# A four-layer conditional network on one core: rotated expert order, spills by block, spread routing

## The reference

```
x += MoE(x):   shared MLP 256->1024->256, gelu(gate)*up, plus the 2 of 8 experts that top-2 of softmax(cond) picks
x += x @ (sum_e cond[b,e] * W1[e] * mask).T + b1        one mixed 256x256 matrix per batch
x += x @ W_base.T + b_base + 2 * sum_e cond[b,e] * (x @ A[e].T) @ B[e].T        LoRA of rank 16
x += down[e](silu(up[e](x)+b) * (gate[e](x)+b)) + b,   e = argmax(cond[b]), hidden 512, 1 of 8 experts
```

## Time and profile before

| what | value |
| --- | --- |
| median of 3 runs | 1271.83 us (1269.04 to 1275.28) |
| the profiled execution's own time | 1274.07 us |
| its span | 1272.4 us |
| granted PE clock, mean | 0.987 of full speed |
| PE / PEld busy | 1224.9 / 1096.2 us |
| DVE / ACT / POOL busy | 643.9 / 476.4 / 476.5 us |
| chain that ended last | PE 84%, POOL 4%, SPq 4%, DVE 3%, issue 3%, DMA 2% |

### The profile page before, as it was taken

One profiled execution on the slowest core, in us unless ns is written; L12 is line 12 of the kernel. 1 busy time (PEld: TensorE's weight loads), 2 busy tenths in 40 slices (PEclk: granted clock), 3 DMA queues, 4 the chain that ended last, 5 costly groups with the idle time before them and its releaser, 6 DMA issues.

```text
span 1272.4 us, 29091 instructions
## 1 busy us (share of the span) xinstructions
PE 1224.9 (96%) x8000; PEld 1096.2 (86%) x8001; DVE 643.9 (51%) x1126; ACT 476.4 (37%) x889; POOL 476.5 (37%) x313
## 2 busy tenths in 40 slices
PE   7987999999999999999999999999999995999998
PEld 6987998888888888888888888999999984887787
DVE  6777575445445455454545454465555542433333
ACT  4354532232322223222322223343344332655554
POOL 2265589307144053260808260010000007888200
PEclk9998999999999999999999999999999997999999
DMA  7258993202112022130313120032233246444211
GB/s 216 61 171 246 278 266 92 67 12 81 47 46 82 14 64 62 33 95 16 95 33 95 44 68 15 19 146 92 99 105 118 85 146 209 148 131 142 64 49 41
DMA packets 130996, 123.82 MB, mean 97 GB/s; under 512 B 64512, under 2 KB 114944, under 8 KB 128896
## 3 DMA queue, kind: packets, MB, share of 16 engines
q1 hardware_dynamic: 114960, 56.56, 16.5%
q0 software_dynamic: 15984, 66.59, 16.1%
HBM read 97.42 MB, written 25.69 MB: 97 GB/s over the span
## 4 chain that ended last, share of the span: by engine, by line
PE 84%; POOL 4%; SPq 4%; DVE 3%; issue 3%; DMA 2%; ACT 1%; POOLq 0%; ACTq 0%; DVEq 0%
PE bank L572 14%; PE bank L573 14%; PE bank L574 14%; PE bank L925 6%; PE bank L624 5%; PE bank L626 5%; PE bank L625 5%; PE bank L609 5%; PE bank L946 3%; PE bank L789 2%; PE bank L668 2%; PE bank L670 1%; PE bank L669 1%; SPq L350 1%; POOL Wl L406 1%
## 5 line engine op out<-in xcount | busy, mean ns | idle before, releaser
L1443 DVE TENSOR_TENSOR FS<-bank,FS 128x512 f32<-128x512 f32 x200 | 138.1, 690 | 273.8 <-PE bank L574 237.5
L404 POOL TENSOR_TENSOR Wh<-raw,one 128x1024 fp32r<-128x1024 f32 x79 | 150.3, 1902 | 316.6 <-PE bank L626 283.4
L1002 ACT ACTIVATE FS<-bank 128x512 f32<-128x512 f32 x200 | 119.5, 597 | 328.7 <-PE bank L574 328.4
L572 PE MATMUL bank<-Wh,RS 128*128 (+1 forms) x576 | 227.0, 394 | 4.7 <-DVE Wl L1533 2.6
L573 PE MATMUL bank<-Wl,RS 128*128 (+1 forms) x576 | 226.5, 393 | 0.0
L574 PE MATMUL bank<-Wh,RS 128*128 (+1 forms) x576 | 225.0, 391 | 0.0
L406 POOL TENSOR_TENSOR Wl<-raw,Wh 128x1024 fp32r<-128x1024 f32 x79 | 191.1, 2419 | 6.2
L624 PE MATMUL bank<-Wh,RS 128*128 (+1 forms) x576 | 174.1, 302 | 0.1
L626 PE MATMUL bank<-Wh,RS 128*128 (+1 forms) x576 | 162.2, 282 | 0.0
L625 PE MATMUL bank<-Wl,RS 128*128 (+1 forms) x576 | 162.0, 281 | 0.0
L1009 ACT ACTIVATE RS<-bank 128x512 fp32r<-128x512 f32 x144 | 86.2, 599 | 172.8 <-PE bank L609 172.8
(11 more groups left out here) (193 smaller groups left out, 2360.5 us busy)
## 6 DMA issues: line engine op xcount, KB each, us to landing
raw<-in_w POOLq DMA_DIRECT2D x87, 512.0 KB, 4.2
mixes<-acc SPq DMA_DIRECT2D x16, 1024.0 KB, 10.8
Wh<-mixes POOLq DMA_DIRECT2D x16, 1024.0 KB, 5.1
FS<-in_xT SPq DMA_DIRECT2D x200, 64.0 KB, 2.3
acc<-in_b SPq DMA_DIRECT2D x8, 640.0 KB, 6.2
acc<-x SPq DMA_DIRECT2D x72, 64.0 KB, 2.2
out_rows<-FS SPq DMA_DIRECT2D x72, 64.0 KB, 2.0
acc<-in_x SPq DMA_DIRECT2D x32, 128.0 KB, 2.9
```

Source lines behind the costliest of these rows:

```text
L404: pool.tensor_tensor(hi, raw[:, k, :], ones_like(PIECE), ALU.mult).then_inc(done, 1)
L572: pe.matmul(ps, ah, bh, start=(i == 0), stop=False)
L1002: act.activation(gl[h], gate_ps[h][:, :], ACT.Gelu_apprx_tanh).then_inc(gelu_done, 1)
L1443: TT(hid[h], up_ps[h][:, :], gl[h], ALU.mult).then_inc(hid_done, 1)
```

## The change

- The 8 turns of the last layer are rotated: the turn order starts with the expert that most batches chose (`rotate3`, on begins and turns), and wraps around. The number of groups stays 36.
- End of the late stage: on PE `down_late(7, 2)` and `(7, 3)` stand ahead of `base(14)`, `turn_x1(15)` behind it, the priming matmuls ahead of `lora(14)`. `lora(15)` stands behind the first `turn_x3`. The first two gathers wait for 15 stores in place of 16, the third for all 16. DVE's `finish(15)` follows the first low part of the last layer.
- Bias loads: six at once when unit 13 has been joined, a seventh one unit later, the eighth behind the first eight gathers, with a semaphore of its own, for which ACT waits ahead of group 4.
- POOL begins to split the last layer's first expert at the count `2 * S1 + 2 * LATE - 2` of `down_done`, when the first half of the shared weights is free, and no longer at `2 * S1 + 2 * LATE`, when all of them are.
- `mixes` lies by block: a spill writes 8 KB in one piece for each partition, and the load of a unit gathers 16 pieces of 512 B for each partition; before it was the other way round. The loads move from POOL's queue to SP's. Each spill is issued by itself, between the token loads.
- The routing work between pairs is cut into seven parts, one at the end of a quarter each (`routing_in_pair`), and DVE's `split_x` moves from the start of a pair to the ends of its first two quarters.
- In `down` of the skill stage, high x high and high x low become one matmul of 512 columns into the two halves of the bank (the high and low weights are now one tile `W`), and low x high stays: two matmuls for a chunk, not three. `add` adds both halves: four instructions for a group, not two, with a semaphore between the pairs.

The diff, changed lines only (deeper indents cut by 8):

```
@@ -74,7 +74,7 @@
-    mixes = nc.dram_tensor("mixes", (NU, P, 2 * PIECE), F32, kind="Internal").ap()
+    mixes = nc.dram_tensor("mixes", (WPIECES, P, NU * P), F32, kind="Internal").ap()
@@ -86,8 +86,8 @@
-Wh = sb("Wh", [P, 2 * EXP0], F32R)
-Wl = sb("Wl", [P, 2 * EXP0], F32R)
+W = sb("W", [P, 2, 2 * EXP0], F32R)
+Wh, Wl = W[:, 0, :], W[:, 1, :]
...
@@ -252,9 +252,14 @@
-        dst = mixes.rearrange("u p (q n) -> q p u n", q=WPIECES)[n]
-        sp.dma_start(dst, staged[n % NSTAGE].rearrange("p (u n) -> p u n", u=NU))\
-            .then_inc(spilled[n % NSTAGE], 16)
+        sp.dma_start(mixes[n], staged[n % NSTAGE]).then_inc(spilled[n % NSTAGE], 16)
+    def load_mix(u, buffer, after=None):
+        if after is not None:
+            sp.wait_ge(l1_done, after)
+        src = mixes.rearrange("q p (u n) -> u p q n", u=NU)[bass.ds(u, 1)].rearrange("a p q n -> p (a q) n")
+        sp.dma_start(mats[buffer].rearrange("p (q n) -> p q n", q=WPIECES), src).then_inc(mix_in[buffer], 16)
@@ -277,24 +282,34 @@
-    for g in range(4, EARLY):
+    def load_shared(g):
-        if g % 2 == 1 and g >= WFIRST + 5:
-            for n in range(2 * (g - WFIRST - 5), 2 * (g - WFIRST - 5) + 4):
-                spill(n)
+    for g in range(4, WFIRST + 4):
+        load_shared(g)
+    for n in range(0, WPIECES - 4, 4):
+        g = WFIRST + n // 2 + 4
+        spill(n)
+        spill(n + 1)
+        load_shared(g)
+        spill(n + 2)
+        load_shared(g + 1)
+        spill(n + 3)
+    spill(WPIECES - 4)
+    spill(WPIECES - 3)
-    for g in range(S0, S0 + 2):
-        load_skill(g, g % 2)
+    load_skill(S0, 0)
+    spill(WPIECES - 2)
+    load_skill(S0 + 1, 1)
-    for n in range(WPIECES - 4, WPIECES):
-        spill(n)
+    spill(WPIECES - 1)
@@ -317,35 +332,42 @@
+    sp.wait_ge(down_done, 2 * S1)
+    load_mix(0, 0)
+    load_mix(1, 1)
+    load_mix(UE, 0, after=2)
+    load_mix(2, 1, after=4)
+    load_mix(UE + 1, 0, after=6)
+        load_mix(k + 1, 1, after=4 * k)
-    store_x3(2 * UL - 4, UE + UL - 3)
-    store_x3(2 * UL - 3, UL - 1)
-    def load_bias3(turns):
+        load_mix(UE + k, 0, after=4 * k + 2)
+    def load_bias3(turns, arrived):
-                         b3[bass.ds(e, 1)].broadcast_to([P, NBIAS])).then_inc(bias3_in, 16)
+                         b3[bass.ds(e, 1)].broadcast_to([P, NBIAS])).then_inc(arrived, 16)
+    store_x3(2 * UL - 4, UE + UL - 3)
+    load_mix(NU - 1, 1, after=4 * UL - 4)
-    load_bias3(range(3))
+    load_bias3((0, 1, 2, 3, 4, 7), bias3_in)
+    sp.wait_ge(x1_done, NU - 1)
+    load_bias3((5,), bias3_in)
+    store_x3(2 * UL - 3, UL - 1)
-    sp.wait_ge(x1_done, NU)
-    load_bias3(range(3, E))
-    store_x3(2 * UL - 1, UE + UL - 1)
-    def gather(i, q, after=False):
+    def gather(i, q, after=None):
-        if after:
-            sp.wait_ge(x3_stored, 16 * NU)
+        if after is not None:
+            sp.wait_ge(x3_stored, 16 * after)
@@ -358,8 +380,14 @@
-    for i in range(NGATHER):
-        gather(i, i, after=i == 0)
+    gather(0, 0, after=NU - 1)
+    gather(1, 1)
+    store_x3(2 * UL - 1, UE + UL - 1)
+    gather(2, 2, after=NU)
+    for i in range(3, NGATHER):
+        gather(i, i)
+    sp.wait_ge(x1_done, NU)
+    load_bias3((6,), bias3_last)
@@ -494,25 +522,10 @@
...
@@ -534,8 +547,9 @@
+    pool.wait_ge(down_done, 2 * S1 + 2 * LATE - 2)
+    expert3_in(0, 2, chosen[0], chosen[1])
-    expert3_in(0, 2, chosen[0], chosen[1])
@@ -619,6 +633,17 @@
+        if not isinstance(e, int):
+            both = out_ps[p].rearrange("p (k n) -> p k n", k=2)
+            for c in range(4):
+                w2_ = W[:, :, bass.ds(at + c * D, D)]
+                if c > 0:
+                    pe.matmul(ps, chunk(hl[h], c), w2_[:, 0, :], start=False, stop=False)
+                mm = pe.matmul(both, chunk(hh[h], c), w2_, start=(h == 0 and c == 0), stop=(h == 1 and c == 3))
+                if c == 0:
+                    pe.matmul(ps, chunk(hl[h], c), w2_[:, 0, :], start=False, stop=False)
+            mm.then_inc(down_done, 1)
+            return
@@ -874,7 +899,10 @@
-        if not last:
+        if last:
+            down_late(k, 2)
+            down_late(k, 3)
+        else:
@@ -884,26 +912,23 @@
-    down_late(UL - 1, 2)
+    turn_x1(NU - 1)
-    down_late(UL - 1, 3)
-    lora(NU - 2)
-    turn_x1(NU - 1)
-    layer1(NU - 1, 1)
-    turn_x2(NU - 1)
+    lora(NU - 2)
+    layer1(NU - 1, 1)
+    turn_x2(NU - 1)
-    lora(NU - 1)
-            pe.wait_ge(x3_done, 2 * NU)
+            pe.wait_ge(z_done, NU)
@@ -963,8 +988,10 @@
+    lora(NU - 1)
+    up_gate3(0, 0, load_expert3(0))
+    pe.wait_ge(x3_done, 2 * NU)
-    up_gate3(0, 0, load_expert3(0))
@@ -1192,11 +1219,8 @@
+    x1_out(NU - 1)
-    x1_out(NU - 1)
-    x2_hi(NU - 1)
-    ranks_hi(NU - 1)
@@ -1243,16 +1267,21 @@
-    act.wait_ge(bias3_in, 16 * E)
+    act.wait_ge(bias3_in, 16 * (E - 1))
+    x2_hi(NU - 1)
+    ranks_hi(NU - 1)
-    with act.Fori(1, G3 // 2 - 1) as pair:
+    step3(2, 0)
+    step3(3, 1)
+    act.wait_ge(bias3_last, 16)
+    with act.Fori(2, G3 // 2 - 1) as pair:
@@ -1336,6 +1365,16 @@
+    largest3, top3, index3, shift3, turns3 = small[:, 232:240], *(small[:, k:k + 1] for k in (240, 241, 242, 243))
+    def rotate3(values, period):
+        done(TT(junk, largest3, values, ALU.mult))
+        done(dve.tensor_reduce(shift3, junk, AX.X, ALU.add))
+        done(TS(values, values, shift3, None, ALU.subtract))
+        done(TS(junk, values, 0.0, None, ALU.is_lt))
+        done(STT(values, junk, period, values, ALU.mult, ALU.add))
@@ -1345,6 +1384,12 @@
+        totals3 = counts[:, 24:32]
+        done(dve.tensor_reduce(top3, totals3, AX.X, ALU.max))
+        first_of(totals3, top3, index3, largest3)
+        rotate3(begins[:, 1, :], ends[:, 1, E - 1:E])
+        done(TT(ends[:, 1, :], begins[:, 1, :], groups[:, 1, :], ALU.add))
@@ -1362,7 +1407,9 @@
+        done(dve.tensor_copy(turns3, turns[:, 1, E - 1:E]))
+        rotate3(turns[:, 1, :], turns3)
@@ -1382,16 +1429,21 @@
...
+    def passed_groups(a):
+        n, k = ((NR0, E - 1), (G3, E))[a]
+        return passed[:, 0:n * k].rearrange("b (n k) -> b n k", n=n), n, k
+    def route_passed(a):
+        v, n, k = passed_groups(a)
+        done(TT(v, iota_slot[:, 0:n].unsqueeze(2).broadcast_to([NB, n, k]),
+                ends[:, a, 0:k].unsqueeze(1).broadcast_to([NB, n, k]), ALU.is_ge))
+        done(TT(v, v, present[:, a, 0:k].unsqueeze(1).broadcast_to([NB, n, k]), ALU.mult))
+    def route_group_turns(a, turn_of):
+        v, n, _ = passed_groups(a)
+        done(dve.tensor_reduce(ended[:, 0:n], v, AX.X, ALU.add))
+        done(TS(turn_of[:, :], ended[0:1, 0:n], float(E - 1), None, ALU.min))
@@ -1404,12 +1456,13 @@
-    def route_tables():
+    def route_sources():
...
+    def route_parts():
...
+    def route_dests():
...
@@ -1426,6 +1480,23 @@
+    def routing_in_pair(pair, q):
+        if (pair, q) == (0, 1):
+            route_passed(0)
+        elif (pair, q) == (0, 2):
+            route_group_turns(0, turn0)
+        elif (pair, q) == (1, 2):
+            route_passed(1)
+        elif (pair, q) == (1, 3):
+            route_group_turns(1, turn3)
+        elif (pair, q) == (2, 1):
+            route_sources()
+        elif (pair, q) == (2, 2):
+            route_parts()
+        elif (pair, q) == (2, 3):
+            route_dests()
@@ -1482,8 +1553,6 @@
-        for p in range(1 if last else 2):
-            split_x(g + 2 + p, p, xset=1 - xset)
@@ -1494,6 +1563,9 @@
+            if q == 1 or q == 2 and not last:
+                split_x(g + 1 + q, q - 1, xset=1 - xset)
+            routing_in_pair((g - FIRST) // 2, q)
@@ -1501,11 +1573,15 @@
-        for j, b in enumerate(batches):
-            half = slice(S * j, S * (j + 1))
-            at = acc[half, bass.ds(b, 1), :].rearrange("p a d -> p (a d)")
-            op = STT(at, out_ps[p][half, 0:D], weight0[half, bass.ds(g - S0, 1)], at, ALU.mult, ALU.add)
-        op.then_inc(acc_done, 1)
+        for part_, done_ in ((0, add_step), (1, acc_done)):
+            if part_ == 1:
+                dve.wait_ge(add_step, g - S0 + 1)
+            for j, b in enumerate(batches):
+                half = slice(S * j, S * (j + 1))
+                at = acc[half, bass.ds(b, 1), :].rearrange("p a d -> p (a d)")
+                op = STT(at, out_ps[p][half, D * part_:D * (part_ + 1)], weight0[half, bass.ds(g - S0, 1)], at,
+                         ALU.mult, ALU.add)
+            op.then_inc(done_, 1)
@@ -1558,12 +1634,8 @@
-    route_experts(0)
-        if i == 0:
-            route_experts(1)
-            route_tables()
@@ -1687,12 +1759,13 @@
+        if last:
+            hidden_lo_late(k, 3)
-        hidden_lo_late(k, 3)
-        if not last:
+            hidden_lo_late(k, 3)
@@ -1701,16 +1774,15 @@
+    join(NU - 1, NU - 1, late=UL - 1)
-    join(NU - 1, NU - 1, late=UL - 1)
-    finish(NU - 1)
@@ -1740,6 +1812,7 @@
+    finish(NU - 1)
```

26 lines of the change are left out of this document (2 added, 24 removed).

## The result

The changed kernel takes 1258.22 us (median of 4 runs, 1253.87 to 1258.96); the kernel before, on the same chip, 1272.19 (1269.04 to 1275.28). The ratio is 0.9883, 95% interval 0.985 to 0.9916. It is faster, by 14.0 us where 27.0 were forecast; the time lies 13 us over the forecast and 0.2 us past the upper end of the range.

What follows compares the result with a forecast made beforehand. PE, dense except for three shared-stage waits, bounds the kernel, and SP's ring of puts and gathers the last layer. 13.7 + 4.9 + 0 + 8.4 = 27.0 us off the profiled 1274.07, median 2.2 lower: forecast 1245, range 1235 to 1258.

Steps and rivals of the forecast that it cites:

- Part 1: Shared stage: spreading the routing and moving `split_x` removes three PE waits and their clock loss, 13.7 us gained, bounds 8 and 17.
- Two such hits inside a quarter, 1.8 us in all: Shared stage: charge for PE waits from slow DVE routing instructions beyond the slack, 1.8 us, bounds 0 and 6.
- The clock term: Shared stage: PE's lower clock behind the three waits goes away, 1.65, 2.0 and 1.65 us, together 5.3 us.
- Rival B: Shared stage keeps half its loss, 7 us, as slow DVE instructions beside POOL make many quarters late: 1252 us, chance 17%.
- Part 2: `down` of the skill stage: merged matmuls save 5.7 us over 544 chunks, less 0.8 us at the end, 4.9 us.
- the merged one 0.2275: 0.0105 us saved: Skill stage `down`: one 512-column matmul takes 0.2275 us where two of 256 columns cost 0.238, per chunk.
- rival D: Skill stage: the doubled add holds DVE past PE's need in each group, slower than before, 1286 us at 0.6 us; 3%.
- Part 3: Mixed matrices loaded by SP: first load about 6 us and hidden, gain 0, bounds 0 and 4 us cost once.
- Part 4: Way into the last layer: the first put comes at 1079.9 in place of 1088.34, 8.4 us earlier, bounds 4 and 11.
- H: Way into the last layer: the time the third gather goes out, 1063.3 us, bounds 1061 and 1068.
- Rival C: Way into the last layer gives nothing, as the bias queue holds `store_x3(13)` and the chain behind: 1253 us, chance 12%.
- Rival A: Last layer: the start gain comes through in full, SP's ring running faster than 5.64 us: 1237 us, chance 12%.

Runs made afterwards that it cites:

- e_unroll: The changed kernel with SP's loop of puts and gathers written out 24 times, nothing left out: 1246.62 us, ratio 0.9796.
- e_one_put: The changed kernel with one put of 128 rows a group in place of two of 64, leaving out the second batch's place: 1238.48 us, ratio 0.973.
- e_before_unroll: The kernel before the change with only SP's loop of puts and gathers written out 24 times: 1260.23 us, ratio 0.99.
- e_old_routing: The changed kernel with routing back in two blocks between pairs and `split_x` back at the start of a pair: 1265.91 us, ratio 0.9958.
- e_after: The changed kernel repeated without any edit, with a second trace: 1258.08 us, ratio 0.9882.
- e_old_down: The changed kernel with the merge in the skill stage's `down` undone, three matmuls per chunk and two adds: 1261.04 us, ratio 0.9913.
- e_old_mixes: The changed kernel with the old DRAM layout of mixed matrices, spills in 512 B pieces and contiguous loads, both by SP: 1260.43 us, ratio 0.9903.

## Why the prediction was right or wrong

- **What bounds the kernel: right.** PE dense, the three waits, and SP's ring in the last layer. e_unroll, e_one_put and e_before_unroll show the last directly. The stall of PE that the prediction named came at its fourth `down3`, but small (1.53 us at 1073.52, where some 8 were forecast): the first `down3` starts at 1057.20, 6.6 us later than the 1066 - 15.4 that the forecast comes to in this trace. The first put is at 1068.90 and 1072.86 in the two traces, where 1061 was forecast.
- **Part 1, "13.7 us gained": the step that failed is "Two such hits inside a quarter, 1.8 us in all", and with it "`route_turns` ... charge 0".** The removed waits were right (12.5 us; e_old_routing has three of them back, 11.3 us). Against them stood 3.2 us of expected waits, and 7.5 and 7.1 came in the two traces. One is a slow instruction of 2.40 us in `route_turns`, which fell on a place with no slack (1.97 us of wait): before, that block ended 0.9 us ahead of POOL's instruction (54.22), and with the added instructions it meets it (52.59). Three are in the tables' routing, close behind each other, which together with another slow one on `RS` between them made 0.80, 2.20 and 0.68 (the last before 120.38). The clock term, 5.3 us, was mis-sized as well: the estimate of e_after gives 152.69 - 12.49 - 136.52 = 3.7 us for the kernel before, though it had a fourth low slice (100 to 105 us, 0.72) that the prediction does not list, and 2.3 of them return in e_after, none in the first trace. The stretch gained 8.7 us in the one trace and 6.8 in the other; undoing it cost 7.8 by the medians. I had seen the cause, and sized it by the mean where the hits come next to each other. Rival B had the cause and about the size, half the gain kept away, but it is half of what is missing in the whole.
- **The charge for `route_places`, 0.9 us: right** (0.66 of wait where there was none).
- **Part 2, 4.9 us: right in size, wrong in its place.** The step "the merged one 0.2275: 0.0105 us saved" did not happen: a chunk of `down` takes (606.82 - 606.11) / 2 = 0.355 us, so the merged matmul takes 0.355 - 0.119 = 0.236, as two of 256 columns do, and the saving is in `up_gate` behind it. That it came to the forecast size is luck. The skill stage is 5.5 us shorter (4.87 in e_old_down against e_after; 5.7 forecast). The 0.8 us charged for the last doubled add were met by luck too: 0.87 us are given back before `turn_x1(0)`, and e_old_down, without that add, gives back 0.91. The four adds cost PE nothing in the loop, so rival D is out. By the medians the merge alone is worth 3.0.
- **Part 3, 0: right for the loads, wrong for the spills.** Loads by SP landed in 6.1 us at the median and `layer1(0)` did not wait. The Trainium skill's warning that row pitches of large powers of two can halve the rate (DMA: Bandwidth & Descriptors, "Latency and other measured facts") shows at most in part: 1 MB apart and in pieces of 512 B, the load of 1 MB took 6.1 to 6.2 us, and 5.1 from one place in e_old_mixes, also by SP; whether the pitch or the size of the pieces makes the 1 us was not tried. The layout as a whole is worth about 2.3 us by the medians, which I had counted as 0 since PE never waited for a spill; by the one profile of the old layout it acts on POOL's loads, whose chain ends the stage. Taking the loads from POOL is the likely source of the 0.9 us before `turn_x1(0)`, which this part did not charge.
- **Part 4, 8.4 us: the rotation was worth that, and the change lost most of it again.** The third gather was forecast for H = 1063.3 in the time of before, and with the 15.4 us that `turn_x2(14)` gained up to there it came at 1067.7 (1052.31 in the trace); from it to the first put 16.6 us were forecast and came. The step that failed is thus the one up to H. The chain that I followed had SP, PE and ACT in it and priced POOL's earlier split at nothing; its cost is the same mechanism that stands in part 1, POOL beside DVE. With the split put back, the stretch from `turn_x1(0)` to the first put is 9.3 us shorter than before (8.1 against e_before_unroll, whose stretch takes 258.0), against 8.4 forecast; with the early split, 3.8 to 4.0. Rival C had the place, half of it, and another cause, the bias queue.
- **Rival A (the ring runs faster once PE is ahead): wrong.** 5.60 us against 5.64. In e_unroll the ring does run faster, by an edit of its own.

In sum, by the medians: routing 7.8, merge 3.0, layout 2.3, rotation 5.6, early split -5.8 makes 12.9 of the 14.0 measured; the rest is within what five rounds can tell.

## What to carry to other kernels

When an engine's work is moved, look at what runs beside it on the engines that it can slow, not only at what waits for it: POOL's split was waited for by nobody, and cost 5.8 us by where it ran. When a stall is cut up, size the leftovers one by one against the slack of the very place that each goes to, and find who waits for the end of the chain. And when one queue's sequencer paces a stage, try the cheapest thing first: writing its loop out gave 11.5 us here, nearly as much as a large change of order.
